# Last layer of a four-layer block on one core: GpSimd works out the routing factors of the third and fourth positions

## The reference

```
x = silu(x_prev * conv_w[:, 0] + x * conv_w[:, 1])
q = silu(x @ Wq); k = x @ Wk; v = x @ Wv; g = x @ Wg      # 16 heads, 8 wide for q and k, 16 for v
q, k = rotary(q), rotary(k)
scores = softmax(v . router_w)                              # two routes
onehot = one_hot(argmax(scores), 2)
norm = 1 / cumsum(onehot over positions)                    # how often the route was chosen so far
qk = (q * scores * onehot * norm) . (k * onehot) * 8 ** -0.5, causal
o = qk @ v
o = (o - mean) / sqrt(var + 1e-5)                           # per head
out = (silu(g) * o) @ Wout
```

## Time and profile before

| | us |
|---|---|
| median of 3 runs | 700.99 (700.14 to 701.1) |
| the profiled execution, its own time | 699.97 |
| its span, first to last instruction | 698.1 |

### The profile page before, as it was taken

One profiled execution on the slowest core, in us unless ns is written; L12 is line 12 of the kernel. 1 busy time (PEld: TensorE's weight loads), 2 busy tenths in 40 slices (PEclk: granted clock), 3 DMA queues, 4 the chain that ended last, 5 costly groups with the idle time before them and its releaser, 6 DMA issues.

```text
span 698.1 us, 13446 instructions
## 1 busy us (share of the span) xinstructions
PE 616.3 (88%) x4521; PEld 489.1 (70%) x4567; DVE 550.7 (79%) x1349; ACT 421.0 (60%) x1371; POOL 272.9 (39%) x370
## 2 busy tenths in 40 slices
PE   3447989989989999999899999999999999999936
PEld 3245767766677777777687777777788778787725
DVE  7997788979676867978888678797864777869697
ACT  4256757766777646666767366668563566663531
POOL 2116564434323644433335534333332355341131
PEclk9578999999999999999999999999999999999987
DMA  9237352342593214333333222324244222010001
GB/s 270 71 145 252 104 157 70 108 159 76 162 315 106 63 53 99 99 99 102 99 112 98 99 99 99 99 99 99 99 159 99 96 103 100 16 31 1 1 0 60
DMA packets 36973, 72.87 MB, mean 104 GB/s; under 512 B 3342, under 2 KB 28586, under 8 KB 32810
## 3 DMA queue, kind: packets, MB, share of 16 engines
q1 hardware_dynamic: 36720, 72.00, 32.9%
q10 hardware_dynamic: 186, 0.02, 0.0%
HBM read 59.41 MB, written 12.60 MB: 103 GB/s over the span
## 4 chain that ended last, share of the span: by engine, by line
PE 58%; DVE 27%; issue 7%; ACT 5%; POOL 2%; DMA 0%; DVEq 0%; ACTq 0%
PE bank L710 13%; PE bank L587 11%; PE bank L690 9%; PE bank L594 6%; PE bank L659 4%; PE bank L734 3%; DVE Cb L1763 3%; PE bank L676 2%; DVE nm L1748 2%; PE bank L691 2%; PE bank L820 1%; PE bank L724 1%; POOL rs L1315 1%; DVE Cb L1778 1%; DVE Cb L1779 1%
## 5 line engine op out<-in xcount | busy, mean ns | idle before, releaser
L710 PEld LDWEIGHTS bank<-V,Pt 128*128 128x128 f32 x1024 | 126.4, 191 | 39.4 <-DVE Cb L1763 26.9
L710 PE MATMUL bank<-V,Pt 128*128 128x129 f32 x1024 | 138.0, 278 | 10.5 <-DVE Cb L1763 9.0
L1065 ACT ACTIVATE square<-bank 128x128 bf16<-128x128 f32 x372 | 98.2, 276 | 69.0 <-PE bank L587 41.0
L690 PE MATMUL bank<-QT,KTt 128*128 128x512 f32 x256 | 132.7, 600 | 2.7 <-POOL diag L1337 2.4
L1048 ACT ACTIVATE Pt<-bank 128x512 f32<-128x512 f32 x128 | 76.7, 599 | 74.4 <-remote 49.2
L1748 DVE TENSOR_REDUCE nm<-bank 128x2 f32<-128x512 f32 x128 | 82.0, 682 | 29.6 <-PE bank L676 29.4
L1315 POOL TENSOR_TENSOR rs<-ve,mhalf 128x6 f32<-128x6 f32 x64 | 94.9, 1483 | 5.3
L1337 POOL TENSOR_TENSOR diag<-identb,nm 128x512 bf16<-128x512 bf16 x64 | 67.0, 1047 | 66.8 <-DVE nm L1748 66.8
L587 PE MATMUL bank<-WQ,xq 128*128 128x256 f32 x512 | 79.1, 297 | 5.3 <-DVE nm L1748 3.1
L1763 DVE SCALAR_TENSOR_TENSOR Cb<-bank,ro,ism 128x128 bf16<-128x128 f32 x256 | 78.1, 347 | 4.5
L587 PEld LDWEIGHTS bank<-WQ,xq 128*128 128x128 f32 x512 | 66.7, 189 | 18.2 <-DVE nm L1748 12.9
(11 more groups left out here) (237 smaller groups left out, 1100.6 us busy)
## 6 DMA issues: line engine op xcount, KB each, us to landing
WQ<-wq_split SPq DMA_DIRECT2D x24, 1024.0 KB, 7.7
WH<-wh_split SPq DMA_DIRECT2D x24, 384.0 KB, 8.9
wq_split<-WQ SPq DMA_DIRECT2D x8, 1024.0 KB, 4.4
ism<-smooth_inverse SPq DMA_DIRECT2D x32, 256.0 KB, 6.4
wst<-in_L_xattn_wproj SPq DMA_DIRECT2D x16, 256.0 KB, 4.1
wh_split<-WH SPq DMA_DIRECT2D x8, 384.0 KB, 3.7
wst<-in_L_xattn_wq SPq DMA_DIRECT2D x8, 256.0 KB, 4.9
wst<-in_L_xattn_wqx SPq DMA_DIRECT2D x8, 256.0 KB, 5.0
```

Of the source, the lines that this page charges most:

```text
L690: nc.tensor.matmul(o[:], KTt[u % 2][:, x, t * P:(t + 1) * P], QT[u % 2][:, x, :], start=True, stop=False)
L710: last = nc.tensor.matmul(o[:, h * (P + 2):h * (P + 2) + P + 1], Pt[:, x, k, h * S + t * P:h * S + (t + 1) * P], V[u % 2][:, x, k, 0:P + 1 ...
L1065: last = A(square[:, t, h], head(t, h), ACT.Square, accum_out=ss[:, t, h:h + 1])
```

## The change

For the third and fourth positions (l of at least `ROUTED` = 2) VectorE no longer computes choice, size and factor. GpSimd does it in a new `route3`, called behind `rotate3(l)`: it writes the choice as plus or minus 0.5 into `sel` and |d| / 2 into `cf`, multiplies the choices of all positions with that of l and turns the product into 0 or 1 (`chosen`), adds these up one position at a time (`number`), gets 1 / number from a polynomial that is exact at 1, 2, 3 (and 4), multiplies by 8 ** -0.5 and the score (`size`), and by `chosen`. VectorE then has one product of `lm` with `chosen` per position, behind a wait for `route_ready`. `head_rstd3` stays in front of that wait in the fourth position. For the first two positions the choice is now written as plus or minus 0.5 as well, with a semaphore `sel_ready`, and the rest is as before. ScalarE's order is unchanged; its tanh for l of at least 2 waits for GpSimd.

```
+        ROUTED = 2
...
-                A(cf[:, l], cf[:, l], ACT.Tanh, scale=0.5).then_inc(s["th_done"], 1)
+                A(cf[:, l], cf[:, l], ACT.Tanh, scale=0.5 if l < ROUTED else 1.0).then_inc(s["th_done"], 1)
...
+            def route3(l):
+
+                i = l - ROUTED
+                one = sel[:, l]
+                pool.wait_ge(s["qkv3_evac"], 3 * NT * (l + 1))
+                chain.add(gp.tensor_scalar(one, dl[:, l], 0.0, -0.5, ALU.is_ge, ALU.add))
+                chain.wait()
+                gp.tensor_tensor(cf[:, l], dl[:, l], one, ALU.mult).then_inc(s["dl_ready"], 1)
+                pool.wait_ge(s["sel_ready"], ROUTED)
+                chain.wait()
+                c, n, f = chosen[i], number[:, i], share[:, i]
+                m = l + 1
+                chain.add(gp.tensor_tensor(c[:, 0:m, :], sel[:, 0:m, :], sel[:, l:l + 1, :].to_broadcast([P, m, NT * H3]), ALU.mult))
+                chain.wait()
+                chain.add(gp.tensor_scalar(c[:, 0:m, :], c[:, 0:m, :], 2.0, 0.5, ALU.mult, ALU.add))
+                chain.wait()
+                chain.add(gp.tensor_tensor(n, c[:, 0], c[:, 1], ALU.add))
+                for k in range(2, m):
+                    chain.wait()
+                    chain.add(gp.tensor_tensor(n, n, c[:, k], ALU.add))
+                chain.wait()
+                low, a0, divisor = ((), 11.0, 6.0) if m == 3 else ((-35.0,), 50.0, 24.0)
+                chain.add(gp.tensor_scalar(f, n, *((1.0, -6.0) if m == 3 else (-1.0, 10.0)), ALU.mult, ALU.add))
+                for a in low:
+                    chain.wait()
+                    chain.add(gp.tensor_tensor(f, f, n, ALU.mult))
+                    chain.wait()
+                    chain.add(gp.tensor_scalar(f, f, a, None, ALU.add))
+                chain.wait()
+                chain.add(gp.tensor_tensor(f, f, n, ALU.mult))
+                chain.wait()
+                chain.add(gp.tensor_scalar(f, f, a0, float(DK3) ** -0.5 / divisor, ALU.add, ALU.mult))
+                pool.wait_ge(s["th_done"], l + 1)
+                chain.add(gp.tensor_scalar(size[:, i], cf[:, l], 0.5, 0.5, ALU.mult, ALU.add))
+                chain.wait()
+                chain.add(gp.tensor_tensor(f, f, size[:, i], ALU.mult))
+                chain.wait()
+                gp.tensor_tensor(c[:, 0:m, :], c[:, 0:m, :], f.unsqueeze(1).to_broadcast([P, m, NT * H3]), ALU.mult
+                                 ).then_inc(s["route_ready"], 1)
+
             for l in range(1, B):
                 rotate3(l)
+                if l >= ROUTED:
+                    route3(l)
...
-                link(v.tensor_scalar(sel[:, l], dl[:, l], 0.0, None, ALU.is_ge))
+                v.tensor_scalar(sel[:, l], dl[:, l], 0.0, -0.5, ALU.is_ge, ALU.add).then_inc(s["sel_ready"], 1)
+                dve.wait_ge(s["sel_ready"], l + 1)
...
+                if l >= ROUTED:
+                    if l == B - 1:
+                        head_rstd3()
+                    dve.wait_ge(s["route_ready"], l - ROUTED + 1)
+                    ch.wait()
+                    link(v.tensor_tensor(lm[:, 0:m, :], lm[:, 0:m, :], chosen[l - ROUTED][:, 0:m, :], ALU.mult))
+                    return
...
-            route3(2)
             weigh3(1)
...
-            route3(B - 1)
             weigh3(2)
```

More of the change, by code:

```diff
@@ L184, in build_program @@
         cnt = lb("cnt", [P, NT * H3])
+        chosen = [lb(f"chosen{i}", [P, B, NT * H3]) for i in range(2)]
+        number = lb("number", [P, 2, NT * H3])
+        share = lb("share", [P, 2, NT * H3])
+        size = lb("size", [P, 2, NT * H3])
         m3 = lb("m3", [P, B, NT * H3])
@@ L300, in build_program @@
             "max_ready diag_ready st_done exp_done pv_done o_evac cq_ready cT2_done catT_evac proj_done x3_ready "
-            "ve3_ready pw3_ready h3_ready h3T_done h3T_evac conv_ready silu_ready proj3_done qkv3_evac rotated dl_ready "
+            "ve3_ready pw3_ready h3_ready h3T_done h3T_evac conv_ready silu_ready proj3_done qkv3_evac rotated dl_ready sel_ready route_ready "
             "th_done sq_ready vs_ready sd_ready sd_done wv3_ready wk3_ready head_rstd_ready og_ready o_ready last_o_ready oT_done oT_evac out_done "
@@ L1888, in dots3 @@
                 ch.add(v.tensor_tensor(pr.rearrange("p (m t c) -> p m t c", m=m, t=NT), k, q, ALU.mult))
-                link(v.tensor_tensor(same[:, 0:m, :], sel[:, 0:m, :], sel[:, l:l + 1, :].to_broadcast([P, m, n3]), ALU.is_equal))
+                if l < ROUTED:
+                    link(v.tensor_tensor(same[:, 0:m, :], sel[:, 0:m, :], sel[:, l:l + 1, :].to_broadcast([P, m, n3]), ALU.is_equal))
+                ch.wait()
                 ch.add(v.tensor_reduce(lm[:, 0:m, :], pr.rearrange("p (m n d) -> p m n d", m=m, d=DK3), AX_X, ALU.add))
+                if l >= ROUTED:
+                    if l == B - 1:
+                        head_rstd3()
+                    dve.wait_ge(s["route_ready"], l - ROUTED + 1)
+                    ch.wait()
+                    link(v.tensor_tensor(lm[:, 0:m, :], lm[:, 0:m, :], chosen[l - ROUTED][:, 0:m, :], ALU.mult))
+                    return
                 link(v.tensor_reduce(cnt[:], same[:, 0:m, :].rearrange("p m n -> p n m"), AX_X, ALU.add))
-                if l == B - 1:
-                    head_rstd3()
                 dve.wait_ge(s["th_done"], l + 1)
```

## The result

| kernel | median us | runs | ratio to before, 95% interval |
|---|---|---|---|
| before | 701.0 (700.04 to 701.66) | 8 | |
| changed | 703.08 (702.08 to 703.39) | 8 | 1.0029 [1.0018, 1.004] |

The account below looks back on a forecast made before the run. VectorE bounds TensorE's hole. Lateness, each step holding the one before, ran 0.6, 3.0, 2.4, 5.2, 5.8 us; 5.7 taken on 699.97 made 705.7 profiled, with 1.02 for the runs' median 706.7 us, range 703.3 to 709.8.

Parts of the forecast that it names:

- third position's mixing starts: VectorE, after waiting 2.8 us for GpSimd's factors and one product: mixing at 673.75, where before it was 673.15, +0.6 us.
- fourth position's factors ready: GpSimd's route for the fourth position: 4.9 us left from 679.4 plus 0.9 lost to the 1024 element product, ready 685.2.
- gate two ends: GpSimd's second gating of outputs, waiting for VectorE's 2048 element product: ends 689.4, making TensorE's second transpose 5.2 us late.
- VectorE's last sum ends: VectorE's sum over the fourth position, behind the long products and gates: ends 691.95, before 689.39, so 2.6 us late.
- end of the span, against before: TensorE's 24 projection matmuls end at 698.7 instead of 692.86, +5.8 us; behind that nothing changes.
- the wait for the factors: Sign: VectorE's product by the third position's factors waits 2 to 3 us for GpSimd.
- the start of the squaring: Sign: ScalarE's squaring of the third position, queued behind the fourth's tanh, starts near 679.6.
- the long rotation: Sign: GpSimd's fourth rotation, pressed between VectorE's mixing products and weighing, has products of 0.7 to 1.9 us each.
- the sum: The prediction's step-by-step timing of the last layer, with TensorE done at 698.7, 5.8 us later than before.
- Gates: GpSimd's gating of positions one to three, colliding with VectorE's long products: ends at 686.4, 689.4 and 691.4.
- Rival (b): GpSimd, once it has the ports, runs its three gates back to back, gate two at 687.4: 704 us, chance 0.12.
- an earlier clock: TensorE's clock back sooner, since it had begun work at 686.4: up to 1.7 us less than the +5.8.

Follow-up runs that it names:

- the run with the shorter chain: Changed kernel with six GpSimd instructions per position instead of 12 and 15, additions and polynomial left out, so no division by the count: 703.23 us, 1.0032 of before.
- the run with the gates held back: Changed kernel with GpSimd's three gates also waiting for VectorE's product of the fourth position's dot products with its factors: 707.25 us, 1.0095 of before.

## Why the prediction was wrong

Step by step, times of the changed kernel less 0.33:

| step | predicted | measured |
|---|---|---|
| third position's mixing starts | 673.75 | 673.77 |
| third variance starts | 680.25 | 680.02 |
| head reciprocal ends | 684.2 | 684.06 |
| fourth position's factors ready | 685.2 | 684.6 |
| gate two ends | 689.4 | 686.7 |
| VectorE's last sum ends | 691.95 | 691.6 |
| end of the span, against before | +5.8 | +2.0 |

The mechanism was right down to the gates: VectorE's waits, the rotation pressed between the mixing products (four of its products took 3.45 us, where they had taken 2.04), the squaring behind the tanh. Of the five signs that the prediction named, the wait for the factors (2.55 us) and the start of the squaring (679.71) came, and the long rotation came for four of its six instructions (its first two took 0.4 us each). The last two did not come: the second gate took 1.10 us and not over 2, and TensorE had no hole between its first two sets of output transposes. The prediction's own conditions for being wrong (rotation over before 676.5, gate two before 686) were set too wide: they ended at 678.7 and 687.0. That the factors were ready within 0.6 us of the sum was partly luck, since the prices of the single instructions were off both ways and cancelled: tensor_tensor 0.25 us at 128x32 (0.23 taken), tensor_scalar 0.22 to 0.33 at 32 and 0.30 at 128 (0.28 and 0.56), the handoff 0.07 to 0.08 as taken. The groups by form of the changed kernel show two of them:

```profile
L1470 POOL TENSOR_TENSOR number<-chosen 128x32 f32<-128x32 f32 x2 | 0.5, 250 | 0.2
...
L1485 POOL TENSOR_SCALAR share<-share 128x32 f32<-128x32 f32 x2 | 0.4, 217 | 0.2
```

The step that failed stands under "Gates": "They now come directly behind and meet the long products. Gate one 685.5 to 686.4; the 2048 element product needs 2.15 us: 688.5; gate two waits for it and ends 689.4". It let VectorE's product by the last factors go first, and gate one behind it. But gate one waits for nothing that is late, so it is ahead of everything that the last factor releases, by 0.08 us. Gate two then gets in ahead of the long product, and only gate three waits, which TensorE needs last. Gate two ended 2.7 us earlier than in my sum.

The order accounts for most of the miss. From the start of the product to the end of the 24 projection matmuls the sum has 13.5 us (685.2 to 698.7), and the run with the shorter chain, whose gates stood in the order of the sum, took 13.6; the changed kernel took 10.1. That is 3.5 of the 3.9 us by which TensorE was done earlier than the sum had it; the rest is the product's start, 0.5 us ahead of the sum. So the price that the sum put on its order was right, and the order was wrong. Rival (b), at 704 and a chance of 0.12, came nearest: it has all three gates back to back, the trace the first two. The range's lower end stood on the same step: it took the collision's order as nearly certain, when a difference of 0.08 us in an estimated start decided over 3 us.

With gate two early, the path is a near tie. TensorE restarts 2.5 us later than before, gets about 0.9 us back by its clock, and loses 0.4 to a wait for VectorE (its last sixteen projection matmuls of the three positions took 3.98 us, 3.62 before): 1.9 us late in all. VectorE's own lateness of 2.2 us, which I had beside the path, is what ends last in the chain of waits; without it, about 1.5 us of TensorE's 1.9 would stand.

The same 3.9 us can be split by time, and there the clock is the smaller part. TensorE's 24 matmuls ended at 695.10 - 0.33 = 694.8, and not at 698.7: 2.7 us of it are gate two's earlier end, 1.2 the time from there on. Eight projection matmuls by the timeline, in the kernel before, the changed one and the one with the shorter chain:

```profile
685.15 3.67 PE L874 MATMUL bank<-Wo,cv 128*128 128x256 f32 x8
```

```profile
688.00 2.85 PE L879 MATMUL bank<-Wo,cv 128*128 128x256 f32 x8
```

```profile
687.84 3.62 PE L879 MATMUL bank<-Wo,cv 128*128 128x256 f32 x8
```

In the changed kernel the granted clock was 0.50 (the low level) from TensorE's restart to 689 and 1.00 from 690 on, where the kernel before had 0.50 for all of its 5.6 us. With the shorter chain, where TensorE idled 1.93 us between its first two sets of transposes, it was 0.50 for 7.4 us (columns as in the earlier trace rows):

```profile
683.90:691.30 7.40, 5.45 (x17) 4.25 (x18) 6.99 (x6) 1.82 (x3) 4.98 (x2) 0.50 0.00 0
```

I had allowed for an earlier clock ("up to 1.7 us less") and took nearly none of it.

## What to carry to other kernels

Handing small work to GpSimd can pay only where VectorE has other work in the meantime: the fourth position's 15 instructions cost no measurable time, the third position's 12 cost 1.7 us, by the wait directly behind them and by the rotation that they pushed into VectorE's long products. When two engines share ports, look at who asks first at each crossing, and let a range hold both orders where the starts are within a few tenths of a us. Here long GpSimd instructions belonged beside VectorE's reductions and reciprocals, not beside its products.

## What the runs showed of the hardware that I had not expected

In the changed kernel's trace an independent GpSimd instruction starts 0.04 us before its predecessor ends (684.91 against 684.95), one that waits for it 0.07 to 0.08 after, and VectorE's, released by the same end, 0.04 after: so the engine that releases another is still ahead of it at the ports. When both wait in turn, the two alternate instruction by instruction: in the run with the gates held back three gates took 6.57 us for 3.2 us of work, and the two 512 element instructions of VectorE beside them 1.43 us each and not 0.69. And GpSimd's cost per element depends on the operation: tensor_scalar with a product and a sum grew by 0.08 us from 32 to 128 elements, tensor_tensor by 0.19. Other forms of tensor_scalar took more at 32 elements already: 0.30 with a sum alone (L1481), 0.32 with a comparison (L1459 at 678.88).
